# Neighbour counts from masks that accumulating DMAs sum during attention, in a two-layer graph kernel

## What is computed

```python
def _L0_gnn_ref(x, adj, ...):
    q, k, v = ...                      # of layer_norm(x) @ w_qkv
    scores = jnp.where(adj != 0, q @ k.T * SCALE, -inf)
    x = x + softmax(scores) @ v @ w_proj + b_proj
    return x + gelu(layer_norm(x) @ w1 + b1) @ w2 + b2

def _L1_gnn_ref(x, adj, Wt, bt, Wa, ba, Wp, bp, gamma, beta):
    h = x @ Wt.T + bt
    s = leaky_relu(h @ Wa.T + ba, negative_slope=0.2)
    scores = jnp.where(adj > 0, s, NEG)
    w = softmax(scores, axis=1)
    y = x + w @ h @ Wp.T + bp
    return gamma * (y - mean) * rsqrt(var + EPS) + beta
```

## Time and profile before

| | us |
|---|---|
| median of 3 runs | 1310.8 |
| lowest, highest | 1310.02, 1312.16 |
| the profiled execution | 1311.44 |
| its span in the trace | 1309.6 |

### The profile page before, as it was taken

How to read it: one execution, slowest core, us unless ns; L and a number is a source line. 1 busy time by engine, 2 the same in 40 slices (tenths; PEclk the granted TensorE clock), 3 DMA queues, 4 the chain that set the end, 5 groups by cost and what they waited for, 6 DMA issues and landing times.

```text
span 1309.6 us, 32088 instructions
## 1 busy us (share of the span) xinstructions
PE 1204.3 (92%) x12034; PEld 349.8 (27%) x12050; DVE 1128.4 (86%) x1647; ACT 1058.1 (81%) x1201; POOL 864.0 (66%) x900
## 2 busy tenths in 40 slices
PE   5654999999999999999999999999999998998997
PEld 3330111111111111111111111111111126874443
DVE  6664999999999999999999999999999994653555
ACT  4553999999999999999999999999999993441000
POOL 5682777777777777777777777777777763440011
PEclk9875999999999999999999999999999998999999
DMA  5001332323332234223332323332233247405860
GB/s 173 1 1 51 126 119 98 114 98 121 122 114 98 98 117 142 98 98 113 113 130 99 114 98 110 121 128 97 98 116 127 83 148 263 137 1 201 292 255 25
DMA packets 41149, 152.49 MB, mean 116 GB/s; under 512 B 5216, under 2 KB 19360, under 8 KB 30752
## 3 DMA queue, kind: packets, MB, share of 16 engines
q1 hardware_dynamic: 36640, 148.26, 31.9%
q10 hardware_dynamic: 4352, 2.10, 0.5%
HBM read 110.50 MB, written 39.85 MB: 115 GB/s over the span
## 4 chain that ended last, share of the span: by engine, by line
ACT 63%; PE 19%; issue 8%; DVE 5%; POOL 3%; POOLq 0%; DVEq 0%
ACT probs L1158 37%; ACT probs L1152 26%; PE ps L786 4%; PE ps L705 2%; PE ps L775 2%; POOL probs L1059 2%; PE ps L714 2%; PE ps L1357 2%; DVE probs L1260 2%; PE ps L763 1%; DVE probs L1198 1%; DVE acc_sb L1268 1%; PE ps L808 1%; PE ps L822 1%; PE ps L679 1%
## 5 line engine op out<-in xcount | busy, mean ns | idle before, releaser
L1260 DVE SCALAR_TENSOR_TENSOR probs<-m,ps 128x512 f32<-128x512 bf16 (+1 forms) x1024 | 928.9, 951 | 36.7 <-PE ps L1357 18.5
L1158 ACT ACTIVATE probs<-probs 128x1536 f32<-128x1536 f32 x512 | 866.7, 1694 | 0.9
L1095 POOL TENSOR_TENSOR probs<-probs,m 128x512 f32<-128x512 f32 x512 | 596.0, 1164 | 229.9 <-ACT probs L1152 200.9
L1370 PE MATMUL ps<-probs,v_sb 128*17 128x512 f32 x4096 | 539.6, 599 | 0.0
L1357 PE MATMUL ps<-kq 32*128 32x512 bf16 x6144 | 427.5, 380 | 39.5 <-DVE probs L1260 9.7
L1152 ACT ACTIVATE probs<-ps 128x512 f32<-128x512 f32 x512 | 410.3, 801 | 26.9 <-PE ps L1357 26.2
L1357 PEld LDWEIGHTS ps<-kq 32*128 32x128 bf16 x6144 | 114.8, 93 | 567.4 <-ACT probs L1152 499.1
L1074 POOL TENSOR_SCALAR m<-adj_in 128x512 bf16<-128x512 int32 x256 | 157.3, 615 | 4.0 <-issue 3.9
L1370 PEld LDWEIGHTS ps<-probs,v_sb 128*17 128x17 f32 x4096 | 68.1, 95 | 217.7 <-issue 210.9
L348 POOL TENSOR_TENSOR probs<-probs,cols 128x2 f32<-128x2 f32 x16 | 11.7, 729 | 110.4 <-DVE probs L625 110.4
L423 ACT ACTIVATE probs<-ps 128x512 f32<-128x512 f32 x8 | 4.8, 597 | 84.1 <-PE ps L763 84.1
(11 more groups left out here) (134 smaller groups left out, 615.1 us busy)
## 6 DMA issues: line engine op xcount, KB each, us to landing
adj_in<-in_adj_t SPq DMA_DIRECT2D x64, 1024.0 KB, 5.7
mask_t<-m SPq DMA_DIRECT2D x64, 512.0 KB, 2.9
kq<-mask_t SPq DMA_DIRECT2D x16, 2048.0 KB, 8.2
attn_t<-acc_sb SPq DMA_DIRECT2D x16, 256.0 KB, 6.6
probs<-in_x SPq DMA_DIRECT2D x8, 256.0 KB, 4.2
tail_words<-attn_t SPq DMA_DIRECT2D x4, 512.0 KB, 3.3
adj_in<-attn_t SPq DMA_DIRECT2D x4, 512.0 KB, 4.4
out<-probs ACTq DMA_DIRECT2D x16, 128.0 KB, 3.7
```

Source lines behind the costliest of these rows:

```text
L1095: nc.gpsimd.tensor_tensor(pr, pr, m01[:, (k // 2) % MRING, :], ALU.mult).then_inc(postmasked, 1)
L1158: nc.scalar.activation(pr, pr, ACT.Exp, scale=UNIT).then_inc(exped, 1)
L1260: nc.vector.scalar_tensor_tensor(out=pr, in0=m.to_broadcast([P, n, CH]), scalar=1.0, in1=ps[:, b:b + n, :], op0=ALU.subtract, op1=ALU.add)\
L1370: last = nc.tensor.matmul(ps[RT * hh:RT * hh + VW, 6 + g, :], v_sb[:, t, h * VW:(h + 1) * VW], probs[:, k % SLOTS, hh // 2, (hh % 2) * CH: ...
```

## The change

During attention, once for each group of four mask tiles, POOL issues a DMA that adds the group's block (128 x 4 x 512 bf16) into a block `counts` of the same shape; the first group of a chunk is copied instead. SP stores the block once per chunk into a new DRAM tensor (`store_counts`). In the tail SP loads each chunk's block back (`load_counts`), and PE counts over its four tiles once per chunk, where before it counted over all 32 mask tiles, 16 in each half. Three semaphores order this: `counted`, `counts_stored`, `counts_in`. To make room, `tail_words` shrinks, acc[0] and xr[0] move from it to the adjacency buffers, and ff moves from `eb` to `wb`; the loaded blocks lie in v_sb and in m01.

```diff
-        tail_words = sb("tail_words", [P, 3840], F32)
+        tail_words = sb("tail_words", [P, 2816], F32)
+        counts = sb("counts", [P, MGROUP, CH], BF16)
...
-        wb = taker(pool_words, v_words)
+        m_words = m01[:, :, :].rearrange("p s q -> p (s q)").bitcast(F32)
+        wb = taker(pool_words, v_words, m_words)
...
-        acc, xr, xb = [lb(2, CH), eb(2, CH)], [lb(SUB, D), eb(SUB, D)], [eb(SUB, D), eb(SUB, D)]
+        acc, xr, xb = [eb(2, CH), eb(2, CH)], [eb(SUB, D), eb(SUB, D)], [eb(SUB, D), eb(SUB, D)]
...
-        ff, hsum, onesf = eb(FF // P, CH), eb(SUB, HID), eb(P)
+        ff, hsum, onesf = wb(FF // P, CH), eb(SUB, HID), eb(P)
...
+        def load_counts(sp, j):
+            if j >= 2:
+                sp.wait_ge(deg_summed, j - 1)
+            sp.dma_start(counts_sb[j % 2], d_dram[j, :, :, :]).then_inc(counts_in[j % 2], 16)
...
+            sp.wait_ge(counts_stored, 16 * NC)
+            load_counts(sp, 0)
+            load_counts(sp, 1)
             for n in range(ERING, 2 * NC):
                 load_edges(sp, n)
+                if n % 2 == 1 and n // 2 < NC:
+                    load_counts(sp, n // 2)
...
-            def degrees(i):
+            def degrees(j):
+                pe.wait_ge(counts_in[j % 2], 16 * (j // 2 + 1))
+                if j >= 2:
+                    pe.wait_ge(deg_copied, j - 1)
+                for t in range(MGROUP):
+                    last = nc.tensor.matmul(ps[t * RT:t * RT + RT, BANK_D[j % 2], :], one_col[:, :],
+                                            counts_sb[j % 2][:, t, :], start=True, stop=True)
+                last.then_inc(deg_summed, 1)
...
             for j in range(2, NC):
-                degrees(2 * j)
                 sums_low(2 * j)
                 project_sums(j - 1)
                 sums_high(2 * j)
-                degrees(2 * j + 1)
+                degrees(j)
                 sums_low(2 * j + 1)
                 project_degrees(j)
                 sums_high(2 * j + 1)
...
+            def store_counts(c):
+                sp.wait_ge(counted, 16 * (NT // MGROUP) * (c + 1))
+                sp.dma_start(d_dram[c, :, :, :], counts[:, :, :]).then_inc(counts_stored, 16)
...
                 if G + 2 < GROUPS:
                     load_adj(G + 2)
+                if G >= per_chunk and G % per_chunk == 0:
+                    store_counts(G // per_chunk - 1)
...
+            store_counts(NC - 1)
             sp.wait_ge(acc_stored, 32 * (NC - 1))
             load_sums(sp, 0)
...
+            def count(G):
+                first = G % (NT // MGROUP) == 0
+                pool.wait_ge(mask_made, MGROUP * (G + 1))
+                if G > 0:
+                    pool.wait_ge(counted, 16 * G)
+                if G > 0 and first:
+                    pool.wait_ge(counts_stored, 16 * (G // (NT // MGROUP)))
+                at = (G % 2) * MGROUP
+                if first:
+                    copy = pool.dma_start(counts[:, :, :], m01[:, at:at + MGROUP, :])
+                else:
+                    copy = pool.dma_start(counts[:, :, :], m01[:, at:at + MGROUP, :], accum_op=ALU.add)
+                copy.then_inc(counted, 16)
...
                 if X >= MRING:
+                    pool.wait_ge(counted, 16 * (G - 1))
...
                 post_mask(k)
+                if k % (2 * MGROUP) == 1:
+                    count(k // (2 * MGROUP))
```

More of the change, by code:

```diff
@@ L47, in gnn_kernel @@
     a_dram = nc.dram_tensor("attn_t", (NC, P, 2, CH), F32).ap()
+    d_dram = nc.dram_tensor("counts_t", (NC, P, MGROUP, CH), BF16).ap()
     shift_dram = nc.dram_tensor("shift_t", (3 * H, N), BF16).ap()
@@ L187, in gnn_kernel @@
         den, aw, ew = wb(SUB), wb(SUB), wb(SUB)
+        counts_sb = [wb(MGROUP * CH // 2).bitcast(BF16).rearrange("p (t q) -> p t q", q=CH) for _ in range(2)]
         BANK_A, BANK_B, BANK_D = (0, 3), (1, 4), (5, 7)
@@ L193, in gnn_kernel @@
         B_FF, B_OUT, B_ACC, B_TURN, B_HID, B_PROJ = 0, 2, 3, 5, 6, 7
+        counted, counts_stored = sem("counted"), sem("counts_stored")
+        counts_in = [sem("counts_in0"), sem("counts_in1")]
         tail_in = sem("tail_in")
@@ L753, in tail_tensor, with sums_low @@
                     hidden(i - 1)
-            def degrees(i):
+            def degrees(j):
[6 more added lines that the diff above has]
+                last.then_inc(deg_summed, 1)
+            def sums_low(i):
                 n = turns[i]
@@ L758, in degrees @@
                 pe.wait_ge(edges_in[i % ERING], 16 * (i // ERING + 1))
[L759 to L770, removed]
                 if half == 0 and j >= 2:
@@ L828, in tail_tensor @@
             pe.wait_ge(x1_made, NC)
-            degrees(0)
             sums_low(0)
@@ L833, in tail_tensor @@
             hidden(NC - 1)
-            degrees(1)
             sums_low(1)
@@ L837, in tail_tensor @@
             pe.wait_ge(h_lo_made, NC)
-            degrees(2)
             sums_low(2)
+            degrees(0)
             column_sums()
@@ L843, in tail_tensor @@
             project_columns()
-            degrees(3)
+            degrees(1)
             sums_low(3)
```

## The result

| | median, us | lowest to highest, us | runs |
|---|---|---|---|
| before, on the same chip | 1311.6 | 1310.02 to 1313.11 | 20 |
| changed | 1304.7 | 1297.92 to 1313.71 | 20 |

The ratio is 0.9954 with a 95% interval of 0.9938 to 0.997: faster by 6.9 us in the medians (6.0 by the ratio), where 12.4 were forecast. The time also spreads over 16 us, where the kernel before spreads over 3. The profiled execution took 1305.56 us (span 1303.8, granted clock 0.966 as a mean).

A forecast was written before the change was run, and what follows sets the result against it. ACT's pace was taken to bound attention and TensorE's matmul chain the neighbour stage at the end. Neighbour stage -13.6 us plus hand-over 1.2 gave -12.4, from the median 1310.8 to 1298.4 us; range 1296.5 to 1305.

The forecast's parts named there:

- TensorE's part: Neighbour stage: 16 degree groups of 0.98 us go, eight of 0.245 us return (bound 382 ns); net -13.7 us.
- The first output: Neighbour stage, chunk 0's output: VectorE is already late, so part of TensorE's gain is lost; 0.1 us allowed.
- Where part of it is given back: Step on chunk 0's first output: TensorE arrives about when VectorE's sum is ready; 0.1 us lost, stage then -13.6 us.
- The loads: Neighbour stage: 4.72 MB per 12.85 us, 367 GB/s, near the ceiling but covered by 25 us of lead; no cost.
- I take 0: Neighbour stage: cost set for the loads, including SP's new wait before load_counts(2); 0 us.
- rival (d): Neighbour stage is bound by its loads after all: 1309 us at 250 GB/s; chance 0.03.
- the 372 scaled from the earlier trace: Neighbour stage: load ceiling in GB/s, scaled from 320 GB/s at a DMA share of 0.86.
- The hand-over: Attention to tail: last accumulating DMA and counts store delay the load of x before turn_acc(0); 1.2 us, 0.6 to 2.0.
- Attention: POOL's 64 DMA issues, 1 us each, fit its 2.76 us idle per eight steps; landing 5.5 us; no cost.
- (a): Accumulating DMA lands after 7 to 11.8 us, delaying load_sums(0) by 2.7 to 7.5 us: say 1302 us; chance 0.13.
- (b): Accumulating DMA sets attention's period when landing takes 11.9 us or more; 1436 us at 14 us; chance 0.08.
- (c): Attention: POOL's DMA issue itself exceeds 2.76 us; 1345 us at 3.5 us, 1371 at 3.9; chance 0.05.

The follow-up runs named there:

- e9: Kernel before, with two output buffers and TensorE's high sums ahead of the projection that waits for VectorE: 1304.48 us, ratio 0.9948.
- e8: e7 with TensorE's high sums ahead of the projection that waits for VectorE: 1291.71 us, ratio 0.985.
- e1: Changed kernel with a second output buffer, so VectorE waits for the stores of two chunks back: 1299.84 us, ratio 0.9912.
- e3: Changed kernel's attention part and hand-over kept, but TensorE counts over all mask tiles as before and loads no counts: 1311.94 us, ratio 1.0005.
- e4: Kernel before, with 512 KB more loaded per chunk in the neighbour stage into a buffer nobody reads: 1311.1 us, ratio 1.0.
- e2: Changed kernel without the loads of counts of chunks 2 to 7, TensorE reusing the first two chunks' counts: 1300.34 us, ratio 0.9915.
- e6: Changed kernel, single output buffer, with 512 KB more loaded per chunk from chunk 2 on: 1306.52 us, ratio 0.9965.
- e7: Changed kernel with two output buffers, three count buffers, four count loads in the neighbour stage, last chunk's counts left in SBUF: 1299.22 us, ratio 0.991.
- e5: Kernel before, with a second output buffer: 1311.03 us, ratio 1.0.

## Why the prediction was right and wrong

**TensorE's part: right, the size of one term off.** The 16 groups of 0.98 us went. Four matmuls of L776 take 0.33 us on the chain (1242.23 to 1242.56), not 0.245: between the quarter and the bound of 0.38. Eight times 0.085 is 0.7 us. By the matmuls alone the gain is 15.7 - 8 x 0.33 = 13.0 us. From the stage's first group to project_degrees(7) the chains of e9 and e8 take 113.40 (1175.46 to 1288.86) and 100.54 us (1174.75 to 1275.29): 12.9. The half chunks aren't all 7.28 us, as the prediction read them: two are 1233.93 - 1219.28 = 14.65 us before and 13.02 to 13.03 now, 1.6 less, so its 14.56 and 12.85 were both a little short and their difference about right.

**The first output: the wait was right, its price was left out.** The step is "Where part of it is given back", which allowed 0.1 us because PE and VectorE both arrive earlier. They do, by the same 2.95 us, and the idle time stays. What it left out is the clock after it, although 5.08 us stand there for matmuls that take 3.40 elsewhere. Between the profiled executions of the kernel before and e1 it makes 1.6 us. But e3 and e4 have the same long stretch at the old pace, so this is not shown to be a cost of the change. That the place as a whole had a price, 5.2 or 6.8 us, is shown by e9 and e8; why the clock stays low for 3.4 us in one execution and 6.8 in another is open.

**The loads: the conclusion "I take 0" was the step that failed.** It asked only whether PE would wait for edges or counts, and it doesn't: rival (d) is refuted, and the core moved 380 GB/s over 40 us and up to 440 in 2 us, above the 372 scaled from the earlier trace rows, which was no ceiling. It didn't ask who else uses those queues. The output's stores do, and behind them stand VectorE and TensorE. Shown: the second buffer brings 4.3 us and the narrow spread (e1), and pace alone and traffic alone bring no wait (e2, e4). e6's profiled execution has two late stores where the changed kernel's has one; one trace of each doesn't show that this is the traffic's doing. Such a store cost 6.0 us in the changed kernel's chain and 4.8 and 2.2 in e6's, by how long TensorE stood idle and whether the clock fell. (The profiled executions of the changed kernel and e1 differ by 1305.56 - 1300.40 = 5.2 us; the first began its neighbour stage 0.8 us earlier.) That the changed kernel's 16 us of spread are zero to three such stores fits the sizes, but only the profiled execution, with one, was seen.

**The hand-over: the path right, its size mostly less.** 1.2 us was taken, bounds 0.6 to 2.0. By the distance from the post-mask of step 505 to turn_acc(0) it is 0.15 us in the changed kernel, 0.55 in e1, 1.54 in e3 and 0 in e7, which goes without it. The load of x took 4.7 to 6.1 us on the chain, where 5.1 was taken. One sum of the prediction is also off by its own working: with a landing after 3.2 us instead of 5.5 the whole 1.2 us would go, not 0.5. From turn_acc to the stage's first group e1 takes 101.77 us, the kernel before 102.26, but e4, with none of the change, 101.86, so these 0.5 us aren't shown to be the change's.

**Attention: right.** Issue 0.87 us for 1, landing 4.6 for 5.5, period unchanged; e3 shows the sum, 1.0005. The wait of the copies (L1093) for the store of the counts was up to 3.6 us where at most 3.0 was worked out, and hidden too. Rivals (a), (b) and (c) are refuted by the same rows. The Trainium skill ("DMA: Bandwidth & Descriptors", Anatomy of one DMA) gave an estimate of 3.2 us for one pass: the plain copy by L1093 lands after 2.9, the accumulating one after 4.6, so that the estimate is 0.3 us off for the first. The second has to read `counts` too; that this is what takes the further 1.7 us wasn't tested.

**Sum, for the change without late stores (before to e1, spans).** 13.0 gained by the matmuls, less 1.6 at the first output, less 0.6 for the later turn_acc, plus 0.5 in the feed-forward stage, is 11.3; measured 1309.6 - 1298.6 = 11.0, in medians 11.2. This adds up two profiled executions; the 1.6 and the 0.5 aren't shown to be the change's. The forecast of 12.4 lies 1.2 us off that. The other 4.3 us of the shortfall are the late stores. The median of 1304.7 us does lie inside the stated 1296.5 to 1305, but by luck: that end of the range stood for rival (a), a late accumulating DMA, which did not happen.

## What to carry to other kernels

When a stage gets faster and its transfers grow, list every DMA that shares the queues, the small stores on other engines too, and follow what stands behind each one's semaphore; a buffer that is free just in time at the old pace is the first to fail. Look at the packets as well as the bytes: a store of 512-byte packets gave way here to one 16 KB packet after each. Price an idle gap of TensorE with the matmuls that follow it at half clock, in which there may be more than in the gap. And when runs of a kernel begin to spread, look in the trace for one rare event: here the spread alone, 16 us instead of 3, told that something other than pace had come in.

## What the runs showed of the hardware that was not expected

- An accumulating DMA inside SBUF, 128 x 2048 bf16 (512 KB), costs POOL 0.87 us to issue and lands after 4.6 us (4.5 to 6.5); the plain copy of the same bytes costs 0.63 and lands after 2.9.
- A store of 128 KB that ACT issues beside SP's loads of 2048 KB landed after 1.8 to 5.4 us before, and after up to 13.8 us in the changed kernel, 14.2 in e6, 14.5 in e7 and 14.0 in e8, with the DMA share at 0.83 to 1.14 in stretches of 2 us behind the changed kernel's store. The Trainium skill ("DMA: Bandwidth & Descriptors", Queues, rings and completion order) says that each DMA engine takes turns between the queues that have work for it, a packet at a time. The trace agrees, and shows that such turns are not even in bytes: one packet of 512 bytes every 0.63 us, with one of 16 KB between. Why in one execution more of a store's packets meet the loads than in another was not found.
- After the same 3.5 us of idle time the granted clock was at half for 3.4 us in two profiled executions at the old pace (before, e5) and for 6.8 in two others (e3, e4). It can fall once work has resumed: before, the projection at 1205.73 still took 1.02 us, its full-clock time, where e1's took 1.84. After 2.13 us of idle time in e6 it did not fall.
